# Moving VectorE's copy of tokens and weights behind the low part of the next tile's rows, in a mixture-of-experts layer after cross-attention

## What is computed

```python
bids = sigmoid(x @ conf_w.T + conf_b) * wealth        # 8 experts
top_bids, selected_experts = top_k(bids, 2)
routing_weights = softmax(top_bids)
def ffn(gw, uw, dw):                                   # inner width 1024
    return (silu(x @ gw.T) * (x @ uw.T)) @ dw.T
output = sum over experts of combine[:, e] * ffn(...)
x = x + tanh(g_ffn) * output
```

## Time and profile before

| | |
|---|---|
| median of 3 runs | 1198.39 us (1196.59 to 1202.21) |
| profiled execution | 1202.42 us, span 1200.6 us |
| TensorE busy | 1091.6 us, 91% of the span |
| VectorE busy | 668.0 us, 56% |
| ScalarE busy | 555.3 us, 46% |
| GpSimd busy | 315.6 us, 26% |
| mean granted clock of TensorE over the span | 0.961 of full speed |

### The profile page before, as it was taken

How to read it: one execution, slowest core, us unless ns; L and a number is a source line. 1 busy time by engine, 2 the same in 40 slices (tenths; PEclk the granted TensorE clock), 3 DMA queues, 4 the chain that set the end, 5 groups by cost and what they waited for, 6 DMA issues and landing times. The chain is left out here.

```text
span 1200.6 us, 24032 instructions
## 1 busy us (share of the span) xinstructions
PE 1091.6 (91%) x8213; PEld 896.2 (75%) x8213; DVE 668.0 (56%) x1588; ACT 555.3 (46%) x891; POOL 315.6 (26%) x366
## 2 busy tenths in 40 slices
PE   5789999999999988289899999999989999999994
PEld 4456666666666655247599999999849999999994
DVE  2546777777777774365644444444564444444442
ACT  3456676666676664155533333333453333333331
POOL 2122444444343332311311122112221122112111
PEclk8899999999999997589999999999999999999998
DMA  8100111111111101384621121112141122112111
GB/s 297 52 15 24 39 37 44 48 46 37 37 37 37 44 30 48 121 317 164 220 56 32 22 36 32 28 30 36 31 140 28 22 36 36 31 23 36 32 26 23
DMA packets 48025, 72.85 MB, mean 61 GB/s; under 512 B 6256, under 2 KB 42864, under 8 KB 44912
## 3 DMA queue, kind: packets, MB, share of 16 engines
q0 software_dynamic: 16896, 43.53, 14.2%
q1 hardware_dynamic: 30000, 27.68, 7.8%
q10 hardware_dynamic: 1088, 1.11, 0.3%
HBM read 47.14 MB, written 24.90 MB: 60 GB/s over the span
## 5 line engine op out<-in xcount | busy, mean ns | idle before, releaser
L1519 POOL DMA_INDIRECT out<-y,token x64 | 104.6, 1634 | 473.1 <-DVE y L1453 364.1
L1379 ACT ACTIVATE silu<-gate 128x512 f32<-128x512 f32 x128 | 76.5, 597 | 277.4 <-PE up L1287 277.4
L1299 PE MATMUL down<-w_split,h_hi 128*128 128x512 f32 x512 | 185.9, 398 | 0.0
L901 DVE TENSOR_REDUCE max_neg<-maxps 128x4 f32<-128x1024 f32 x128 | 156.4, 1222 | 52.8 <-PE maxps L510 51.1
L1287 PE MATMUL gate<-x_hi,w_split 128*128 128x256 f32 x1024 | 184.5, 282 | 0.0
L1287 PE MATMUL up<-x_hi,w_split 128*128 128x256 f32 x1024 | 183.8, 281 | 0.0
L1444 DVE TENSOR_TENSOR h<-silu,up 128x512 f32<-128x512 f32 x128 | 88.0, 688 | 171.4 <-ACT silu L1379 171.4
L703 ACT ACTIVATE probs<-scores 128x1024 f32<-128x1024 f32 x124 | 127.8, 1030 | 60.5 <-PE scores L535 60.5
L1287 PEld LDWEIGHTS gate<-x_hi,w_split 128*128 128x128 f32 x1024 | 148.8, 188 | 3.0
L1287 PEld LDWEIGHTS up<-x_hi,w_split 128*128 128x128 f32 x1024 | 147.8, 188 | 0.0
L1301 PE MATMUL down<-w_split,h_lo 128*128 128x256 f32 x512 | 144.2, 282 | 0.0
(11 more groups left out here) (164 smaller groups left out, 1756.3 us busy)
## 6 DMA issues: line engine op xcount, KB each, us to landing
xg<-dispatched SPq DMA_DIRECT2D x41, 272.0 KB, 2.8
stage<-gate_T POOLq DMA_DIRECT2D x8, 1024.0 KB, 7.5
stage<-up_T POOLq DMA_DIRECT2D x8, 1024.0 KB, 9.4
stage<-down_T POOLq DMA_DIRECT2D x8, 1024.0 KB, 12.0
x_all<-x SPq DMA_DIRECT2D x16, 256.0 KB, 6.3
ctxT<-ctxT SPq DMA_DIRECT2D x16, 256.0 KB, 2.7
out<-x_all SPq DMA_DIRECT2D x16, 256.0 KB, 2.1
out<-y,token POOLq DMA_INDIRECT x72, 3.8
```

The costliest lines, as they stand in the source:

```text
L901: V.tensor_reduce(to, maxps[:], AX.X, ALU.max, negate=True).then_inc(s["max_taken"], 1)
L1299: mm(down[t][:].rearrange("p (n d) -> p n d", n=2), h_hi[:, i, rows], split[:, :, cols], start=i == 0, stop=False, skip_group_check=True)
L1379: nc.scalar.activation(silu[pair % 2][:], gate[pair % 2][:], ACT.Silu).then_inc(s_silu, 1)
L1519: pool.indirect_dma_start(out, bass.IndirectOffsetOnAxis(token[:, t:t + 1], axis=0), y[:, t, :], None, compute_op=ALU.add).then_inc(s_adde ...
```

## The change

In VectorE's `next_rows`, the call that makes the next tile's `x_lo` moves from behind the two copies to the head of the function, ahead of the waits for the adds. `next_rows` is used by short and long tiles alike, 40 times in an execution. No instruction is added or taken away, and no other engine's program is touched.

```diff
             def next_rows(r, n, firsts):
 
+                rest_of_rows(n + 2)
                 dve.wait_ge(s_noted, n + 1)
                 if firsts > 0:
                     dve.wait_ge(s_added, r * (16 * TT) + 16)
                 if firsts > 1:
                     dve.wait_ge(s_first_added, 16 * (firsts - 1))
                 V.tensor_copy(token[:], noted_token[:])
                 V.tensor_copy(weight[:], noted_weight[:]).then_inc(s_moved, 1)
-                rest_of_rows(n + 2)
                 dve.wait_ge(s_moved, n + 1)
                 dve.wait_ge(s_down, n + 1)
```

## The result

The changed kernel takes 1204.05 us (median of 22 runs, 1196.99 to 1208.97) against 1199.39 us for the kernel before (22 runs, 1195.94 to 1203.96): a ratio of 1.0034, 95% interval 1.0022 to 1.0046, so some 4.1 us slower. That is less than the 0.5% by which the prediction set its chances, yet the interval leaves out 1: it is a small loss and not noise. The forecast was 1199.9 us, +1.5 us, with a range that ends at 1204.5 us. One profiled execution took 1205.59 us, with a span of 1203.8 us.

A forecast was written before the change was run, and what follows sets the result against it. TensorE, busy 1091.6 of 1200.6 us, was taken as the bound. A gain of 0.9 us from earlier rows and a clock loss of 2.4 us made +1.5 us on 1198.39 us: 1199.9 us, range 1194.5 to 1204.5 us.

The forecast's parts named there:

- both places: Short first tiles of experts 3 and 5, after long tiles; TensorE waited 3.00 and 2.65 us for `x_lo` behind late adds.
- the forecast's own band: Net change with the stop moved to the rows' wait: -1.2 us (no clock loss) to +3.4 us (no gain); chance 78%.
- Parts 1 and 2: 32 long tiles and 6 undelayed short tiles: VectorE's copies fit into idle time or a 0.70 us gap; cost 0.
- Part 3: Places 1 and 2: `x_lo` ready before TensorE needs it, stall goes; 5.00 and 5.58 us gained if nothing else were late.
- Part 4: Row transposes at both places: `xg` loads still late, TensorE waits 4.5 and 5.1 us; 0.45 us gained each, 0.9 us total.
- The page's rule of part 4: DMA engines go round queues packet by packet, so rows issued earlier land earlier by as much, taken as 0.45 us.
- Part 5: Behind the new stops before the transposes, TensorE at 1.2 GHz loses 1.2 us a place, 2.4 us together; bounds 0 and about 4.
- A: Rival: rows land within 4.2 us of issue, both places gain in full, 10.6 us, giving 1187.8 us; chance 8%.
- C: Rival: the edit does nothing to speak of, as other executions' adds or waits differ; time stays 1198.4 us; chance 9%.
- B: Rival: new stops bring 8 us of slow clock, 4 us lost at each place; +7.1 us, 1205.5 us; chance 5%.

The follow-up runs named there:

- the kernel with own buffers: Changed kernel with token, weight and y buffers of their own for short tiles, so copies wait for short tiles' adds only; 1.0022 of the kernel before.
- both filled kernels: Changed kernel plus further TensorE matmuls at two places: 9 and 11 before row transposes, 1.0041; 4 and 5 there, 1.0034; 3 and 4 at tile head, 1.0015.
- the two places timed alone: Kernel before with the new order in one short tile only: expert 3's (place 1) 1.0015, 1.8 us slower; expert 5's (place 2) 1.0019, 2.3 us slower.
- the one with own buffers and late weights: Changed kernel with short tiles' own buffers and GpSimd's weight loads issued behind the short tile's add; 0.9974 of the kernel before, 3.1 us faster.

## Why the prediction was right, and where its steps were off

It was right in its outcome, "no change" by its own bound of 0.5% and inside its range, and in the mechanism of both places; but the time is 4.1 us up and not 1.5. That lies outside the forecast's own band of -1.2 to +3.4 us, and inside the range only by the 3 us added for the spread of runs, which is luck in part: the sum left out a term of over 2 us.

- *Parts 1 and 2, tiles without a late add:* right. VectorE still idles 1.09 us ahead of `y_rest` in long tiles, and outside the three stretches the stage is as long as before.
- *Part 3, the stall that goes:* right; TensorE passed both places without a stop.
- *Part 4, what is late next:* right in kind and nearly in size: stops of 4.31 and 5.13 us where 4.5 and 5.1 us stood. Its gain of 0.45 us a place was wrong. From the token copy to the next note it takes 586.16 - 584.88 = 1.28 us after, and as much before, where the note came at

```profile
588.02 0.17 DVE L1422 COPY noted_token<-xg 128x2 int32<-128x2 int32 x1
```

  and 588.02 - 586.74 = 1.28 us. `x_lo` had stood in time that VectorE's queue needs anyway: without it 0.47 us of idling stand there. And an earlier issue would have gained nothing: the kernel with own buffers shows the rows landing at a moment that the weights set, within 1.5 us. The gain is 0, the lower bound, and at the row transposes the changed kernel is where the kernel before was.
- *The page's rule of part 4* (the Trainium skill, "DMA: Bandwidth & Descriptors", Queues, rings and completion order) was read as an earlier landing for an earlier issue. These runs do not bear out that reading: issued 2.8 us earlier, the rows landed at the same 87.4 us. How the engines go round their queues no run here shows.
- *Part 5, the clock:* the term that was mis-sized. I took 1.2 us a place out of bounds of 0 and 4. The stretch from the row transposes to the end of `down` takes 4.6 us at full clock (both filled kernels) and 6.29, 6.86, 7.31 and 6.22 us in the changed kernel: 2.1 us a place, against 4.6 to 5.1 us at the places in the two traces of before. I had allowed for a slow stretch that passes inside the stop; it did not.
- *Missing:* the stop ahead of expert 7, 2.49 and 2.84 us, in none of the rivals. The trace of before has no such stop, and the prediction looked for none behind the two places.

Of the rivals, A (rows land at once) came true only once the weights were moved; C did not; B had the right mechanism, and half its price.

Two clock losses of 2.1 us and the stop of 2.7 us make 6.9 us, more than the 4.1 us measured. The sum charges the new order in full and the old one with nothing; the old one has stops and slow stretches of its own, which differ from one execution to the next. Taken as whole stretches, the traces give 2.1, 1.3 and 2.6 us, 6.0 us; the two places timed alone, 1.8 and 2.3 us, are the better account of the time. The rest of the gap stays open.

**Open.** Whether TensorE waits for that packet of code ahead of expert 7, and why it starts late. All four traces with the old order at place 2 lack the stop; of the ten with the new one eight have it, and the two without are the one with 9.6 us of further matmuls in that tile and the one with own buffers and late weights. The packet of code tells all fourteen apart, but what makes it start early in some and late in others no run shows. That the old order's stop at the head of expert 6's tile gives TensorE's queue time to fetch its code is a guess that fits most of them and not all.

## What to carry to other kernels

When a wait is taken off an in-order queue's front, follow what stays behind it: here the note that frees the only row buffer still stood behind the same add, so the bound engine stopped half a tile later, for longer. An earlier issue was worth nothing where the transfer shared the DMA engines with 3 MB issued just before; with the big transfer ordered behind the small urgent one, the edit paid. Price a stop of TensorE by where it stands as well: behind the new stops the clock was half for 3 to 6 us, which costs little beside a wait to come and is paid in full in front of work.

## What I had not expected of the hardware

- Behind stops of 2.65 and 3.00 us TensorE's granted clock fell in the first trace of before; behind 2.42 and 2.89 us it stayed at 1.00 in the second. Behind 0.77 and 1.28 us the matmuls ran at full pace, and behind 3.7 to 5.1 us, at all ten places with the new order and a late landing and nothing to fill the stop, at the slow one.
- A load of 272 KB, issued 2.4 or 4.6 us behind the last of 3 MB of weights, landed at the same moment of the stage, 10.6 and 7.8 us after its issue; with the weights issued behind it, it took 2.9 us.
- TensorE stood still for 1.8 to 3.3 us ahead of a short tile behind an empty loop, for nothing that the timeline names. The DMA view's packets of the kind "instruction" point at code that comes late: with branch hints the seven stops end 3.7 to 4.0 us after such a packet of 16 KB starts.
